# Four layers on one core: three stages normalise their own input, and the gated products are unrolled

## The reference

```python
def _L1_xattn_ref(x, context, ln_g, ln_b, cln_g, cln_b, Wq, Wkv, Wo, Wff1, Wff2):
    xn = layer_norm(x, ln_g, ln_b)               # 16 heads of 64; one key/value head
    ...
    out = attention(xn @ Wq, kv of layer_norm(context)) @ Wo
    ff = xn @ Wff1
    h, gate = (ff[..., :FF_INNER], ff[..., FF_INNER:])
    return out + jax.nn.silu(gate) * h @ Wff2    # the gated products
def _L1_ffn_ref(x, W1, b1, W2, b2, scale):       # gelu MLP of width 512, low-rank terms from tokens 1 to 16
def _L2_xattn_ref(x, context, bias, W_q, W_k, W_v, W_out, b_out):
    scores = q @ k * atten_scale + bias * 2.0 ** -(head + 1)   # 16 heads of 64 with keys of their own
    return softmax(scores) @ v @ W_out + b_out
```

## Time and profile before

| | |
|---|---|
| median of 3 runs | 1849.66 us |
| profiled execution, in all | 1855.54 us |
| its span, first to last instruction | 1853.7 us |
| PE busy | 1561.6 us, 84% of the span |
| PE weight loads busy | 997.7 us, 54% |
| DVE busy | 1199.7 us, 65% |
| ACT busy | 885.2 us, 48% |
| POOL busy | 663.4 us, 36% |
| mean granted clock of PE | 0.927 |

### The profile page before, as it was taken

The page is one execution under the profiler, slowest core; times in us unless marked ns, Lnnn a source line. Parts: engine busy times, 40 slices in busy tenths (PEclk is TensorE's granted clock), DMA queues, the critical chain, the costliest instruction groups (busy, mean ns, idle before and its releaser), DMA issues. The chain is left out here.

```text
span 1853.7 us, 29578 instructions
## 1 busy us (share of the span) xinstructions
PE 1561.6 (84%) x10155; PEld 997.7 (54%) x10155; DVE 1199.7 (65%) x2484; ACT 885.2 (48%) x2473; POOL 663.4 (36%) x619
## 2 busy tenths in 40 slices
PE   5998858699799997979999889999855589489998
PEld 2565535455577765533333367777633234367776
DVE  4897562488678865438988966666676467723333
ACT  3664432277565552237677645566521244233332
POOL 2557340224554423138888942222501300300000
PEclk9999977799999999979999989999987799579999
DMA  6000000000000000020000000000000000000000
GB/s 267 2 2 2 1 1 1 0 1 2 1 1 2 2 1 1 1 81 1 0 1 1 1 1 1 1 1 2 1 1 0 1 1 1 0 1 1 0 0 23
DMA packets 2725, 18.84 MB, mean 10 GB/s; under 512 B 544, under 2 KB 672, under 8 KB 1696
## 3 DMA queue, kind: packets, MB, share of 16 engines
q1 hardware_dynamic: 2592, 17.14, 2.3%
HBM read 16.09 MB, written 1.05 MB: 9 GB/s over the span
## 5 line engine op out<-in xcount | busy, mean ns | idle before, releaser
L727 POOL TENSOR_TENSOR l_xattn_probs<-l_xattn_probs,l_xattn_recip 128x512 f32<-128x512 f32 x128 | 140.9, 1101 | 271.0 <-DVE l_xattn_recip L711 271.0
L895 ACT ACTIVATE l_attn_probs<-ps,l_attn_neg_max 128x128 f32<-128x128 f32 x512 | 144.7, 383 | 81.9 <-DVE l_attn_neg_max L944 81.4
L2409 POOL TENSOR_TENSOR l_mamba_hc<-l_mamba_h,l_mamba_c 128x512 f32<-128x512 f32 x128 | 158.9, 1267 | 0.0
L2311 DVE TENSOR_TENSOR_SCAN l_mamba_h<-ps,l_mamba_dBx 128x512 f32<-128x512 f32 x128 | 152.7, 1212 | 1.8 <-ACT ps L2208 0.7
L2081 PE MATMUL ps<-l_mamba_hc,w_const 128*128 128x512 f32 x256 | 136.6, 637 | 19.5 <-POOL l_mamba_hc L2409 16.5
L3080 DVE SCALAR_TENSOR_TENSOR xn<-ps,l_moe_gates,xn 128x128 f32 x224 | 63.1, 344 | 138.4 <-PE ps L3004 138.4
L3050 ACT ACTIVATE l_moe_hidden<-ps,w_early 128x512 f32<-128x512 f32 x112 | 70.7, 683 | 117.1 <-PE ps L2986 117.1
L3004 PEld LDWEIGHTS ps<-w_early,l_moe_hidden 128*128 128x128 f32 x896 | 109.6, 194 | 29.5 <-issue 21.6
L3004 PE MATMUL ps<-w_early,l_moe_hidden 128*128 128x128 f32 x896 | 110.2, 277 | 4.6 <-ACT l_moe_hidden L3050 4.6
L2986 PE MATMUL ps<-xnT,w_early 128*128 (+1 forms) x224 | 108.1, 609 | 0.0
L245 POOL TENSOR_TENSOR rs<-rs,neg_half 128x12 f32<-128x12 f32 (+2 forms) x22 | 36.7, 1669 | 195.6 <-DVE rs L239 195.6
...
## 6 DMA issues: line engine op xcount, KB each, us to landing
...
```

Source lines behind the costliest of these rows:

```text
L727: nc.gpsimd.tensor_tensor(probs[:, t % 4, :, :], probs[:, t % 4, :, :], along(recip[:, t % 2, :], [P, 4, P]), ALU.mult)\
L895: ins = nc.scalar.activation(probs[:, t % 4, g, :], S_of(t)[:, g * P:(g + 1) * P], ACT.Exp, bias=neg_max[:, t % 2, g:g + 1], accum_out=total)
L2311: nc.vector.tensor_tensor_scan(flat(h[:, t % 2, half, :, :]), G.ps[:, DA_BANK[half], :], flat(dBx[:, t % 2, half, :, :]), 0.0, ALU.mult, A ...
L2409: nc.gpsimd.tensor_tensor(heads4(hc[:, t % 4, half, :]), h[:, t % 2, half, :, :], c_sb[:, t % 3, :, :], ALU.mult).then_inc((hc0_set, hc1_s ...
```

## The change

The block `layernorm` of l1_xattn, l1_ffn and l2_xattn goes; its work is done inside the sublayer's own block by a new class `Lead`. Quads 0 and 1 are transposed ahead of the steps (in l2_xattn the product with b_out and the projection k0 come even before quad 0), quads 2 and 3 after the scores of steps 1 and 3, and ACT copies them at its steps 2 and 4. DVE normalises its late tiles at step 1. In l1_ffn quad 2 is transposed behind the first `prepare(1)` and quad 3 behind `up(1)`; the products with `even_at` move from `prepare` into `up` (`place_rows`). The output product of the attention is split in two halves, each with a wait and a signal of its own. In l2_xattn the projection k0 comes before q0, and the bias tiles are made four to a step in the first four steps. `Wkv.since` starts its quads at steps 4, 24 and 43 (5, 23, 41 before), inverts from k = 12 and divides at k = 20. The gated products are written out chunk by chunk, with two output banks and two sets of `hidden`; the variances of the first 12 tiles and six of their normalised tiles now stand behind the last multiplication on DVE (they stood at the second chunk of the last quad, with eight tiles behind the last multiplication), and POOL normalises two (three before). `halves` stays False for both attentions.

```diff
--- before.py
+++ after.py
...
-    def early(self, eng, ops, me):
+    def early(self, eng, ops, me, q=None):
         for b in range(self.applied, self.first):
-            if self.share(b, me):
+            if self.share(b, me) and q in (None, b // QUAD):
                 normal(ops, self.G, b).then_inc(self.normed[me], 1)
...
+class Lead:
+    def __init__(self, nc, G, s, weights, banks, gT=None, bT=None):
+        self.nc, self.G, self.weights, self.banks, self.gT, self.bT = nc, G, weights, banks, gT, bT
+        self.spent, G.spent = G.spent, []
+        for handle in G.cleared:
+            nc.release_semaphore(handle)
+        G.cleared = []
+        begun, G.begun = G.begun, None
+        self.rest = Rest(nc, G, s, begun)
+        self.turned, self.stored = s.sem("lead_turned"), s.sem("lead_stored")
+    def sync(self, sp):
+        clear_spent(self.nc, self.G, sp, self.spent)
+    def needs(self, eng):
+        eng.wait_ge(self.G.loaded[self.weights], 16)
+    def tensor(self, pe, q):
+        nc, G = self.nc, self.G
+        self.rest.wait_normed(pe, q)
+        if self.banks[q] in self.banks[:q]:
+            pe.wait_ge(self.stored, q)
+        for j in range(QUAD):
+            mm = nc.tensor.transpose(G.ps[:, self.banks[q], j * P:(j + 1) * P], G.xn[:, q * QUAD + j, :], G.c["ident"])
+        mm.then_inc(self.turned, 1)
+    def scalar(self, act, q):
+        nc, G = self.nc, self.G
+        act.wait_ge(self.turned, q + 1)
+        dst, bank = G.xnT[:, q * QUAD:(q + 1) * QUAD, :], heads4(G.ps[:, self.banks[q], :])
+        if self.gT is None:
+            nc.scalar.copy(dst, bank).then_inc(self.stored, 1)
+        else:
+            nc.scalar.activation(dst, bank, ACT.Identity, bias=self.bT, scale=self.gT).then_inc(self.stored, 1)
+    def wait(self, eng, b):
+        eng.wait_ge(self.stored, b // QUAD + 1)
...
+        lead = Lead(nc, G, s, cfg.tag, (2, 3, 5, 5), gT, bT)
...
+                if name[0] == "q":
+                    lead.wait(pe, b)
...
+                if t == 1:
+                    lead.wait(pe, QUAD)
...
+                if t == 0:
+                    lead.wait(pe, NB - 1)
...
-            def finish(b):
-                pe.wait_ge(o_copied, 2 * (b + 1))
-                wait_taken(pe, place["out", b] - 2)
-                for c in range(8):
+            def finish(b, half):
+                pe.wait_ge(o_copied, 2 * b + half + 1)
+                if half == 0:
+                    wait_taken(pe, place["out", b] - 2)
+                for c in range(4 * half, 4 * half + 4):
                     mm = nc.tensor.matmul(ring("out", b)[:, 0:P], oT[:, b % 2, c, :], cfg.w["o"][:, c * P:(c + 1) * P],
                                           start=c == 0, stop=c == 7)
                 mm.then_inc(out_made, 1)
+            lead.needs(pe)
             if cfg.b_out is not None:
                 nc.tensor.matmul(G.ps[:, T_BANK, 0:P], G.c["ones_row"], cfg.b_out, start=True, stop=True).then_inc(b_made, 1)
             for n in range(n_proj):
+                if names[n] == "q0":
+                    lead.tensor(pe, 0)
                 project(n, 0)
+            lead.tensor(pe, 1)
             for t in range(STEPS + V_LAG + 2):
                 if t < STEPS:
                     scores(t)
-                    for n, name, b in at_step(t):
-                        project(n, b)
+                    if t == 1:
+                        lead.tensor(pe, 2)
+                    if t == 3:
+                        lead.tensor(pe, 3)
+                    if not cfg.halves or finished(t) is None:
+                        for n, name, b in at_step(t):
+                            project(n, b)
...
-            after(act, out_made, b - 1)
+            after(act, out_made, 2 * (b - 1))
...
+            lead.needs(act)
+            lead.scalar(act, 0)
             for n, name in enumerate(names):
                 take(act, "A", n, name, 0)
+            lead.scalar(act, 1)
...
+                    if t in (2, 4):
+                        lead.scalar(act, 1 + t // 2)
...
+            lead.rest.early(dve, nc.vector, 0, 0)
+            lead.rest.variances(dve)
+            for q in range(1, NQ):
+                lead.rest.early(dve, nc.vector, 0, q)
             for n, name in enumerate(names):
                 take(dve, "V", n, name, 0)
+            if cfg.bias_ready:
+                lead.needs(dve)
+            def add(b):
+                dve.wait_ge(out_made, 2 * (b + 1))
+                if cfg.b_out is not None and b % QUAD == 0:
+                    dve.wait_ge(x_ready, b // QUAD + 1)
+                nc.vector.tensor_tensor(G.x[:, b, :], G.x[:, b, :], ring("out", b)[:, 0:P], ALU.add).then_inc(added, 1)
+                if ahead:
+                    dve.wait_ge(added, b + 1)
+                    ahead.stats(b)
             for t in range(STEPS + V_LAG + 3):
+                b = finished(t - 1)
+                if b is not None and cfg.halves:
+                    add(b)
+                if t < U and cfg.bias_ready:
+                    cfg.bias_ready(dve, t)
...
+                if t == 1:
+                    lead.rest.late(dve, nc.vector, 0)
...
-        return [(q, t - 5 - 18 * q) for q in range(NQ - 1)]
+        return [(q, t - start) for q, start in enumerate((4, 24, 43))]
...
-            if k == 22:
+            if k == 20:
...
-            if 13 <= k < 13 + self.PIECES:
-                self.invert(dve, q, slice((k - 13) * (QT // self.PIECES), (k - 12) * (QT // self.PIECES)))
+            if 12 <= k < 12 + self.PIECES:
+                self.invert(dve, q, slice((k - 12) * (QT // self.PIECES), (k - 11) * (QT // self.PIECES)))
...
+            def up(n):
+                q, c = n // CH, n % CH
+                after(pe, multiplied, n - 1)
+                for bank, chunk in ((2 * (c % 2), CH + c), (2 * (c % 2) + 1, c)):
+                    mm = nc.tensor.matmul(G.ps[:, bank, :], w["wff1"][:, chunk * P:(chunk + 1) * P],
+                                          G.xnT[:, q * QUAD:(q + 1) * QUAD, :], start=True, stop=True)
+                mm.then_inc(made, 1)
 
             def down(q):
                 pe.wait_ge(multiplied, CH * (q + 1))
-                after(pe, added, q)
+                after(pe, added, q - 1)
                 for j in range(QUAD):
                     for c in range(CH):
-                        mm = nc.tensor.matmul(G.ps[:, 4, j * P:(j + 1) * P], hidden[:, c, j * P:(j + 1) * P],
+                        mm = nc.tensor.matmul(G.ps[:, OUT[q % 2], j * P:(j + 1) * P], hidden[:, q % 2, c, j * P:(j + 1) * P],
                                               w["wff2"][:, c * P:(c + 1) * P], start=c == 0, stop=c == CH - 1)
                 mm.then_inc(out_made, 1)
 
-            up(0, (0, 1))
-            with pe.Fori(0, NQ - 1) as q:
-                up(q, (2, 3))
-                up(q + 1, (0, 1))
-                down(q)
-            up(NQ - 1, (2, 3))
-            down(NQ - 1)
+            for n in range(NQ * CH + 2):
+                if n < NQ * CH:
+                    up(n)
+                if n >= CH and n % CH == 1:
+                    down(n // CH - 1)
 
         @block.scalar
         def _(act):
-            with act.Fori(0, NQ) as q:
-                for c in range(CH):
-                    act.wait_ge(made, CH * q + c + 1)
-                    if c < 2:
-                        act.wait_ge(multiplied, CH * q)
-                    else:
-                        act.wait_ge(multiplied, CH * q + c - 1)
-                    nc.scalar.activation(gate[:, c % 2, :], G.ps[:, 2 * (c % 2), :], ACT.Silu).then_inc(gated, 1)
+            for n in range(NQ * CH):
+                act.wait_ge(made, n + 1)
+                after(act, multiplied, n - 1)
+                nc.scalar.activation(gate[:, n % 2, :], G.ps[:, 2 * (n % 2), :], ACT.Silu).then_inc(gated, 1)
 
         @block.vector
         def _(dve):
-            def body(q):
-                for c in range(CH):
-                    dve.wait_ge(gated, CH * q + c + 1)
-                    after(dve, out_made, q)
-                    nc.vector.tensor_tensor(hidden[:, c, :], gate[:, c % 2, :], G.ps[:, 2 * (c % 2) + 1, :],
-                                            ALU.mult).then_inc(multiplied, 1)
-                    if q == 0:
-                        for half in range(2):
-                            wkv.scan(dve, LAST, c, half)
-                    if q == 1 and c < 2:
-                        wkv.sum(dve, LAST, c)
-                    if 2 <= CH * q + c - 4 < 2 + QUAD:
-                        j = CH * q + c - 6
-                        wkv.invert(dve, LAST, slice(j * P, (j + 1) * P))
-                    seen_behind(dve, ahead, added, q, c)
-                if q == NQ - 1:
-                    ahead.apply(dve, nc.vector, 8)
+            def add(q):
                 dve.wait_ge(out_made, q + 1)
                 x = G.x[:, q * QUAD:(q + 1) * QUAD, :]
```

(65 more changed lines are left out.)

75 lines of the change are left out of this document (43 added, 32 removed).

## The result

The changed kernel takes 1831.3 us in the median of four runs (1828.7 to 1836.8), beside 1852.3 for the kernel before in the same comparison: the ratio is 0.990, with a 95% interval of 0.987 to 0.993. In a second comparison, of six runs against ten, it took 1828.1 beside 1850.2: 0.988 (0.986 to 0.990). So it is faster by 1.0 to 1.2%.

The account below looks back on a forecast made before the run. PE was taken to fill the wide attention stages and gated products, so only stretches where PE stands could give gains; the terms sum to -17.1 us, from the 1849.7 median to 1832.6, stated as 1833, range 1824 to 1845.

Parts of the forecast that it names:

- seam 1: Last statistics of l1_attn to first scores of l1_xattn: 7.4 us shorter at full clock, 5.3 at 1.2 GHz.
- first steps of l2_xattn: Late transposes, copies and waits in the first steps cost 2.8 us by the scores of step 5; ends 1.2 and 4.
- Rival A: The clock falls at all three starts, since first projections come with short gaps: 5 us lost, 1838; chance 0.16.
- Seam 3: Last statistics before l2_xattn to its first scores: 5.4 us shorter, 3.4 with half clock for four us.
- Seam 2: Last statistics before l1_ffn to its first hidden tile: 4.2 us shorter; 1.2 paid back for quads 2 and 3.
- Gated products: PE's holes of 1.47 and 1.46 us in the gated products go: 3.0 us gained; the third hole's time stays.
- Scans: Moving the recurrence's scans in l1_xattn so only one step holds scan and inversion: 1.5 us gained, ends 0 and -2.2.
- Ends: Half of each attention stage's last output runs during the wait for its second half's copy: 1.4 us gained for both.
- B: Rival: first steps pay back more, with one further copy wait in each attention stage; sum -8.4 us, 1841; chance 0.16.
- C: Rival: the swap of k0 and q0 in l2_xattn reaches the path, 26 us over 15 tiles; 1859; chance 0.06.
- D: Rival: the loops' unrolling and split outputs leave the holes in place, 4.4 us back; 1837; chance 0.06.
- E: Rival: every term at its better end and the scans' relief in full; 1826; chance 0.08.

Follow-up runs that it names:

- The kernel with fillers: Changed kernel plus unread identity transposes on PE, 16 behind its last l1_attn work and 8 ahead of q0 in l1_xattn: seam 1 took 5.32 us instead of 6.42.

## Why the prediction was right, and where it was off

The sign was right and so were most of the mechanisms; two steps were not, the clock at seam 1 and the cost of the first steps of l2_xattn. That the time came out within 2 us is in part luck, as the sum at the end of this section shows. By its own steps:

- **Seam 1, -7.4 (half clock -5.3).** Measured -6.6, with q0 and q1 at low clock. The kernel with fillers shows the full-clock value: 13.04 - 5.32 = 7.7. The sum had taken full clock because "the pauses shrink to under 2 us"; this step failed. Rival A was right here.
- **First steps of l1_xattn, +1.8.** Measured +2.2, by the kernel with the old scans. Inside the ends of 1.0 and 3.5.
- **Seam 3, -5.4 (half clock -3.4).** Measured -6.7 at full clock, and 15.4 - 11.1 = -4.3 in the profiles at low clock. The scores came at 8.7 where the sum had 10. Half of the difference is q1: the sum had it start 5.1 us after the last statistics, 0.7 behind q0, for the copy of k0, and it started after 4.4 with a wait of 0.20. The other half is in the products behind it, which took 4.3 us and not 4.9.
- **First steps of l2_xattn, +2.8.** Measured +3.8. This is the mis-sized term. "DVE's bias tiles, 0.14 each, and 1.0 of late normalisation stay inside its slack of one step" was wrong: four tiles take 2.55 instead of 0.6, because two of them stand until an operation of POOL ends, and three normalisations 1.62 instead of 1.0, because one of them does; without the tiles the steps are 1.5 us shorter. PE's waits for ACT's copies, "about 0.5 and 0.6", were 0.61 and 1.40. The ceiling of 4 held.
- **k0 ahead of q0, 0.** Right: 15.65 us per tile in either order.
- **Seam 2, -4.2.** Measured -4.1, at low clock, which the sum had weighted by half; at full clock it is 13.36 - 8.00 = -5.4. The paid-back part, +1.2, was +1.4.
- **Gated products, -3.0.** Measured -4.2 in the stage: the end of the third down comes 3.55 us earlier (the two holes are 2.9 of it; the rest is up products that take 7.03 instead of 7.17 and start 0.16 before the down products' last piece ends), and the tail is 11.4 where the sum had 11.8 and the kernel before 12.0. Late next was, as said, the chain over POOL: with it shortened, PE is last. Not seen was that the seam behind loses 1.3 with the new stage. Net -2.9.
- **Scans, -1.5.** Measured -2.3, just past the better end of -2.2. The prediction had let part of it come back by itself; nothing did.
- **Ends, -1.4.** 0.75 and 0.73, so -1.5. But the end of l2_xattn had 2.7 us of low clock, which is in no step.

Of rivals, B was partly true (first steps +6.0 instead of +4.6), C, D and E not. The misses have both signs: the steps give -17.1 and the touched stretches -15.3. Without the 2.7 us at the end of l2_xattn the measured steps would give -18.0. Brought to the baseline, -15.3 would be 1849.7 - 15.3 = 1834.4. In the two comparisons the medians differ by 21.0 and 22.1 us, so about 6 us more have gone than the touched stretches explain, in medians too. The forecast of 1833 against 1831.3 hides this: the kernel before was 2.6 us slower in that comparison than the baseline of the sum, and the 6 us are in no step.

In the pair of profiles they are in untouched code, 4.0 of them in l2_mamba. Its first 56 us in the changed kernel and in the kernel with early variances, where the whole sublayer took 281.1 and 286.6 us:

```profile
776.69:832.69 56.00, 45.13 (x120) 20.74 (x120) 31.35 (x60) 29.49 (x49) 26.05 (x23) 0.88 0.17 67
```

```profile
777.92:833.92 56.00, 45.39 (x108) 20.90 (x109) 26.98 (x55) 26.61 (x44) 21.51 (x19) 0.76 0.17 67
```

In the same 56 us PE works through 120 pieces in one and 108 in the other, at a clock of 0.88 and 0.76; the kernel before had 0.79 and 285.1. Over all 14 profiles the code up to the last statistics of l1_attn takes 466.5 to 476.4 us, l2_mamba 280.4 to 286.6, what lies behind l2_xattn 510.8 to 516.9. Whether the change makes the shorter of these more frequent, or the six and ten runs fell so, stays open: the kernel before has one profile only.
